# Top-k attention with counted thresholds on one core: ScalarE's PSUM copies placed ahead of its counting pass in a slot

## What is computed

```python
h = tok(x)                                  # DFT power, mel filters, log, DCT, projection
qkv = (layernorm(h) @ w_qkv).reshape(B, N, 3, HEADS, HEAD_DIM)      # B=16, N=250, 12 heads of 16
attn = jnp.einsum('bhnd,bhmd->bhnm', q, k) * SCALE
kth = jax.lax.top_k(attn, 100)[0][..., -1:]
attn = jnp.where(attn >= kth, attn, -jnp.inf)
out = jnp.einsum('bhnm,bhmd->bhnd', softmax(attn), v)
h = h + out @ w_proj + b_proj
h = h + moe_top2_of_8(layernorm(h))         # L0_ffn
h = h + performer_relu_attention(layernorm(h))
h = h + moe_top8_of_16(layernorm(h))        # L1_ffn
```

## Time and profile before

| | |
|---|---|
| median of the three runs shown | 2680.43 us (2673.62 to 2687.41) |
| the profiled execution: its time | 2691.15 us |
| its span, first to last instruction | 2689.1 us |
| mean granted TensorE clock in it | 0.862 of 2.4 GHz |
| PE busy / share | 2431.5 us / 90% |
| DVE busy / share | 1836.2 us / 68% |
| ACT busy / share | 1527.3 us / 57% |

### The profile page before, as it was taken

How to read it: one execution, slowest core, us unless ns; L and a number is a source line. 1 busy time by engine, 2 the same in 40 slices (tenths; PEclk the granted TensorE clock), 3 DMA queues, 4 the chain that set the end, 5 groups by cost and what they waited for, 6 DMA issues and landing times.

```text
span 2689.1 us, 39761 instructions
## 1 busy us (share of the span) xinstructions
PE 2431.5 (90%) x11650; PEld 2052.7 (76%) x11650; DVE 1836.2 (68%) x6330; ACT 1527.3 (57%) x4856; POOL 72.7 (3%) x45
## 2 busy tenths in 40 slices
PE   7778789989998999999998977999997999999999
PEld 3446677777777787877777766878886999999898
DVE  3258899999999999999999998734442322222223
ACT  2398888888788878879888763211111222222222
POOL 0000000000000000000000000000000101110110
PEclk9975578888788878868877778999997999999999
DMA  3000000000010000000000000220000000000000
GB/s 124 0 1 1 1 17 18 14 21 16 13 21 18 18 16 17 17 16 19 19 13 20 16 20 16 47 83 0 0 0 1 4 7 3 6 6 6 3 6 10
DMA packets 34998, 44.09 MB, mean 16 GB/s; under 512 B 6054, under 2 KB 33676, under 8 KB 34060
## 3 DMA queue, kind: packets, MB, share of 16 engines
q1 hardware_dynamic: 32208, 38.57, 5.6%
q10 hardware_dynamic: 2592, 3.33, 0.4%
HBM read 38.43 MB, written 3.20 MB: 15 GB/s over the span
## 4 chain that ended last, share of the span: by engine, by line
PE 44%; DVE 34%; ACT 9%; issue 8%; POOL 2%; DVEq 1%; DMA 1%; another core or an unknown queue 0%; SPq 0%; ACTq 0%; POOLq 0%
PE bank L465 20%; PE bank L714 7%; ACT late L927 5%; DVE late L1362 4%; DVE late L1359 3%; DVE late L1385 3%; PE bank L544 3%; DVE late L1355 3%; DVE late L1247 2%; DVE late L1469 2%; DVE late L1365 2%; DVE extra L1496 2%; PE bank L579 2%; POOL arena L447 2%; PE bank L775 2%
## 5 line engine op out<-in xcount | busy, mean ns | idle before, releaser
L927 ACT ACTIVATE late<-arena,late 125x250 bf16<-125x250 f32 x1152 | 561.5, 494 | 0.0
L1562 DVE TENSOR_TENSOR pair<-pair,arena 128x500 f32<-128x500 f32 x192 | 138.9, 724 | 444.9 <-PE bank L714 354.4
L465 PE MATMUL bank<-xT,late 128*128 128x250 f32 x1536 | 360.8, 377 | 0.0
L579 PEld LDWEIGHTS bank<-vaug,late 125*125 125x125 f32 x1536 | 241.3, 231 | 153.5 <-ACT late L937 139.3
L579 PE MATMUL bank<-vaug,late 125*125 125x17 f32 x1536 | 233.7, 288 | 106.3 <-ACT late L937 105.4
L1041 ACT ACTIVATE pair<-bank 128x500 f32<-128x500 f32 x192 | 112.7, 587 | 382.0 <-PE bank L465 381.9
L544 PE MATMUL bank<-late 16*125 16x251 f32 x768 | 295.8, 519 | 20.6 <-ACT arena L904 19.7
L465 PEld LDWEIGHTS bank<-xT,late 128*128 128x128 f32 x1536 | 286.9, 192 | 26.3
L714 PE MATMUL bank<-late,pair 128*125 128x192 f32 x1536 | 280.4, 326 | 0.0
L714 PEld LDWEIGHTS bank<-late,pair 128*125 128x125 f32 x1536 | 258.3, 187 | 9.2
L465 PE MATMUL bank<-extra,w_b_g 128*128 128x250 f32 x768 | 261.9, 474 | 2.4 <-DVE late L1469 2.4
(11 more groups left out here) (182 smaller groups left out, 3867.6 us busy)
## 6 DMA issues: line engine op xcount, KB each, us to landing
late<-comb_rows SPq DMA_DIRECT2D x128, 125.0 KB, 2.9
late<-comb_rows SPq DMA_DIRECT2D x128, 62.5 KB, 2.6
late<-in_d SPq DMA_DIRECT2D x1, 3072.0 KB, 10.2
out_h<-extra ACTq DMA_DIRECT2D x16, 187.5 KB
late<-in_d SPq DMA_DIRECT2D x1, 2304.0 KB, 15.2
arena<-in_frames SPq DMA_DIRECT2D x1, 1562.5 KB
w_b_g<-in_b_g SPq DMA_DIRECT2D x1, 1536.0 KB
w_b_u<-in_b_u SPq DMA_DIRECT2D x1, 1536.0 KB
```

Of the source, the lines that this page charges most:

```text
L465: ins = pe.matmul(dst, lhs(t), rhs(t), start=t == 0, stop=t == 1)
L579: ins = pe.matmul(bank[4][0:P, at:at + VW], pT[:, s % 2, kh, half * P:half * P + P], vaug[:, p, kh, UH * g + s, :], start=kh == 0, stop=kh ...
L927: ins = sc.activation(mk[:, n_par(u), t, :] if k == 3 else junk[:, t, :], s_sb[:, ub, t, 0:N], ACT.Sign, bias=thr[:, (n_par(u) + k + 1) % ...
L1562: dv.tensor_tensor(hid[:, s % 2, :, :], gl[:, s % 2, :, :], c, ALU.mult).then_inc(hid_set[1], 1)
```

## The change

In ScalarE's hand-written order of a slot, the copy of scores (`a_s`) and the copy of transposed weights (`a_pt`) trade places with each other and both go ahead of the counting pass of slots 1, 2 and 3. Nothing is added or removed; the four other engines keep their order.

```diff
                 if g == 0 and s == 0 and has(i - 3):
                     o_copy(0, i - 3, bank[0])
-                if s and unit(i, g, p, 4 - s):
-                    a_count(unit(i, g, p, 4 - s), 3 - s)
+                if new:
+                    a_s(new, s)
                 was = (old, s - 2) if s >= 2 else (last, s + 2)
                 if was[0]:
                     a_pt(*was)
-                if new:
-                    a_s(new, s)
+                if s and unit(i, g, p, 4 - s):
+                    a_count(unit(i, g, p, 4 - s), 3 - s)
                 if s == 2 and after:
                     a_qk(after)
```

## The result

The changed kernel takes 2718.89 us (median of 4 runs, 2712.55 to 2727.04) against 2682.15 us for the kernel before in the same comparison. The forecast was 2682 in a range of 2660 to 2700; the time lies outside it, on the side of rival B.

What follows compares the result with a forecast made beforehand. VectorE was taken to set the pace from about 400 us, a ScalarE, PE, ScalarE loop before. Terms -3 + 3 + 2 = +2 us on the profiled 2691.15 gave 2693, carried to the median 2682, range 2660 to 2700.

Steps and rivals of the forecast that it cites:

- rival B: Slower: VectorE stalls in a_steps behind the late count of slot 3; +20 us, 2700; chance 0.21.
- Item 1: Steady part: PE's L579 no longer waits for the count; -3 us, bounds 0 and -8.9.
- Item 2: Slot 3: count ends at S + 4.92 (S: PE's scores end), sometimes late for a_steps; +3 us, bounds 0 and +9.6.
- Item 3: Seven early periods, one walked at low clock: 26.7 us where it was 26.47; +2 us, bounds -17 and +18.
- item 4: ScalarE, slot 0: later count covered by a_steps, so no cost; without that cover 22 us.
- edits that cost nothing: Title of item 4: ScalarE's reordering in slot 0 was to add no time.
- Rival A: Faster: early loop shortens as PE runs at 2.4 GHz; about -20 us, 2660; chance 0.14.

## Why the prediction was wrong

**What bounds the kernel** was right: VectorE from 400 us on, the loop through L579, L565 and L544 before. It was right too that PE's 67.8 us would go (0.7 left) and that they would bring little.

**Item 1** (-3 us) came out at its size in the waits that it named. VectorE's waits for PE were 8.9 us and are 4.7 at L1416 and 0.8 at L1496, 5.5 us: -3.4. As time it is not confirmed: the kernel with only the transposed weights ahead has the same freedom of PE and a steady part within 0.3 us of before.

**Item 2** (+3 us, bound +9.6) is the step that failed: 26.9 us of waits for ScalarE where there were 1.8, and 28.8 us of time in the steady part. Its formula was right, as the period that ends at 1028.58 shows on PE, ScalarE and VectorE:

```profile
1021.30 0.19 PE L555 MATMUL bank<-ones_col,late 125*1 125x1 f32 x2 [1.89 <-ACT late L887]
1021.41 2.03 PE L544 MATMUL bank<-late 16*125 16x251 f32 x4
...
1023.48 0.58 ACT L904 COPY arena<-bank 125x502 f32<-125x502 f32 x1 [1.14 <-PE bank L544]
...
1028.23 0.19 ACT L927 ACTIVATION_READ_ACCUMULATOR late<-arena,late 125x1 f32 x1
...
1028.48 0.06 DVE L1115 MEMSET carrier<- 1x1 f32 x1 [1.67 <-remote]
```

S is 1021.41 + 2.03 = 1023.44, plus 4.92 is 1028.36; the count's last read ends at 1028.42 and VectorE begins a_steps at 1028.48, 1.67 us late. What was wrong is the step "PE's times will not stay: the 1.8 us a period of item 1 make S earlier", and with it the bound of +9.6, which held PE's times where they were. S became later, by a wait that the sum did not hold: L555 for the copies of queries and keys, which stand behind the count of slot 2, which itself had been made to wait. Both orders printed ahead of the prediction show it: L555 ahead of L544 on PE, L886 and L887 behind L927 on ScalarE. I had called L555 a small product and looked at its duration, 0.19 us, and not at what it waits for.

**The same item missed the square root.** VectorE waits for L980 in slot 3 in the same clip's periods. By the run that moved it, this was a place where lateness shows and not a cost of its own.

**Item 3** (+2 us) failed for the same reason: the seven periods take 7.5 us more. It was walked step by step and can be checked so. The wait in slot 2 was given as 2.6 us and is there with 2.38; the flag's wait of 1.71 us in slot 3 was not in the walk. With the flag behind the copies of queries and keys, which end at about 20.0 in the walk, the scores of slot 3 end at 22.1, their copy starts at 22.2 in place of 20.8, and the period is 26.7 + 1.4 = 28.1 us; it measured 28.04. The multiplication by seven was wrong too: before the change the seven took 26.47, 26.47, 29.18, 31.20, 31.79, 24.61 and 31.38 us, so only the first two are the period that was walked. The fifth took 31.80 after the change, so it was bound by something else. ScalarE in the period from 223.92:

```profile
230.86 0.58 ACT L904 COPY arena<-bank 125x502 f32<-125x502 f32 x1 [0.25 <-PE bank L544]
235.71 0.89 ACT L945 ACTIVATE late<-arena,late 125x250 f32<-125x250 f32 x2
238.97 0.58 ACT L904 COPY arena<-bank 125x502 f32<-125x502 f32 x1 [2.38 <-PE bank L544]
```

The walk also had L579 wait for the copy of transposed weights behind the one of scores, but priced the swap in item 4 by slot 0 alone. The run that took the swap back returned 29 of the 38 us, so "edits that cost nothing" is the second step that failed.

**Rival B** (0.21) had the right place, a_steps behind a late count that hangs on the scores of its own slot, but neither the flag nor the order of the copies. Its price was 20 us, the loss 38: it too rested on the periods that were late with PE's times held. Its sign, over 15 us of idle ahead of a_steps, was half there: 12.1 us there and 14.8 at the square root.

**Rival A** did not come: the granted clock between 200 and 300 us was 0.55. Its early period of 24.1 us was reached, but by the kernels that copy the transposed weights first, and at a granted clock of 0.57, not by a clock above 0.7. In the changed kernel PE's waits at L579 went, its idle time between 400 and 1600 us fell from 106 to 84 us, and the clock fell from 0.80 to 0.76. By the rule of the Trainium skill named in the prediction (TensorE: Matmul & The Clock Gate, Part 1: The HAM clock gate) fewer idle gaps should have held the clock or raised it; this case's traces do not agree. Since the same work is busy for longer at a lower clock, the busy times do not say what led the clock down.

## What to carry to other kernels

When an instruction is moved ahead on an in-order engine, list for each instruction that it now delays who waits for it, and follow each of those until the walk comes back to the moved instruction or leaves it for good; a cheap instruction with a wait (here 0.19 us of PE) can close a loop. Put ahead of a long independent pass only what is ready when it stands there: the copy whose input was ready first was worth 0.4%, and the one whose input came last turned 3.9 us of work without dependences into a link of the loop. Margins read with the other engine's times held are only good as long as nothing that the moved work feeds stands ahead of what they are counted from.

## What was not expected

The amount of idle time told little. ScalarE waited 41.1, 172.3 and 192.3 us for the scores between 400 and 1600 us in three kernels whose ratios to the first are 1, 1.0023 and 1.0142, so the first 131 us more go with 0.2% and the next 20 us with 1.2%. The first figure is a sum of two things, as PE was freed in the same step: against the kernel with only the transposed weights ahead it is 0.6%. The second surprise is the size of the single misplaced copy: with the scores ahead and the transposed weights behind, the same instructions take 3031.83 us, 13% more, from the swap of two copies of 0.5 us around a count.
